# Routing the first share of tokens in the drain of attention, with a larger share and blank matmuls in every step

## The chip, the cores and the metric

The kernel runs on one core of one Trainium2 chip. The metric is device time in microseconds (us) of one execution, the median of several runs. A difference under about 2% (11 us here) counts as no difference.

## The reference

Sixteen sequences of 256 tokens with 128 features go through one post-norm attention layer with 16 heads of 8 features, and then through a mixture of experts, each with a residual and a layer norm.

```python
q, k, v = heads(x @ Wq.T + bq), heads(x @ Wk.T + bk), heads(x @ Wv.T + bv)
attn = softmax(q @ k.T / sqrt(8)) * head_mask
x = layernorm(x + (attn @ v) @ Wo.T + bo)              # x: 16 x 256 x 128
probs = softmax(x @ Wr)                                # 8 experts
gate = top-2 of probs, divided by their sum
routed = sum over e of (gelu(x @ Wfc[e] + bfc[e]) @ Wproj[e] + bproj[e]) * gate[:, e]
shared = gelu(x @ Wfc_s + bfc_s) @ Wproj_s + bproj_s
x = layernorm(x + shared + routed)
```

The kernel computes only the two chosen experts of each token: the token's row is sent to two slots of a table in HBM, sorted by expert, and the expert stage works through that table.

## The kernel before

Four stages follow each other, each with its own instruction queues and a barrier of all engines between them.

**Attention** (`build_attention`). One batch is one sequence. A software pipeline of 20 steps (`STEPS = BATCHES + 4`, t = 0 to 19) works on several batches at once. In step t the batch `now` = t-1 has its raw scores made by TensorE and its row maxima taken by VectorE (`largest`, 16 reductions, L554). The batch `late` = t-2 has its shifted scores made by TensorE, into a ring of two PSUM buffers (`ring_ps`), and exponentiated by ScalarE (`exp_pair`, 8 of them). The batches `last` = t-3 and `gone` = t-4 are normalised, projected and put through the layer norm (`add_residual`, `take_stats`, `take_mean` on VectorE, `make_x1` on GpSimd). The order on every engine is written out by hand, as a step function; TensorE's runs over eight pairs p = 0 to 7 of heads. Everything that uses the ring takes its place in it in TensorE's order: an entry can begin when the entry two places before has been evacuated by ScalarE. From step 17 on no batch is `now` (no maxima), from step 18 on none is `late`; steps 17 to 19 are called the drain here.

In between stands work for the second half of the layer. In odd steps GpSimd cuts four finished tiles of 128 tokens (`halve`), in even ones from 6 to 18 TensorE turns them (`turn`, p = 2) and makes their router logits (`find_logits`, p = 6). `keep_clock(n)` puts n blank matmuls of 512 columns in TensorE's queue, behind the projection of v at p = 2 and behind `turn_heads` at p = 6 in the steps of `KEPT`, and at other places in steps 0 to 2 and in the drain.

**Routing** is done by share (`SHARES`, in tiles; share 0 within attention, share 1 in the next stage). `Router.pick` finds the two best experts, TensorE counts the tokens of each expert (`share_counts`), `reserve` and `rank` turn counts into slots, `gate` makes the weights, `place` gives each token's slot, `shift_on` and `end_on` carry the state to the next share. All are small VectorE instructions, each of which waits for the one before it (`then`). `Placer.send` then issues one indirect DMA from GpSimd for each tile and each of the two choices (L1357), 64 in all. `PLACED` says how many go out within attention, at two places of a step; the rest go in the next stage.

**Shared expert** (`share_and_place`). TensorE, ScalarE and VectorE do the shared expert's 32 tiles (VectorE: `low`, L1534, and `add`, L1539). GpSimd does nothing but the sends that are left. The stage ends when every one of the 64 has landed.

**Routed experts** (`routed_experts`), 39 blocks of 256 slots, and **add and normalise**.

Of the kernel before, what the change touches and what calls it, by code (L numbers as in the profile page):

```python
# [14 lines left out]
HEADS = 16  # L15
# [17 lines left out]
SHARES = ((0, 16), (16, 32))  # L33
PICK_STEP, COUNT_STEP, PLACE_STEP = 13, 14, 15
TURNED_EARLY = 7
PLACED = {15: (0, 3), 16: (2, 3), 17: (2, 3), 18: (2, 2)}
# [4 lines left out]
KEPT = range(13, 17)  # L41
STEPS = BATCHES + 4
PROBS = 6
Q_AT, K_AT, TURN_AT, LOGIT_AT, COUNT_AT = 0, 3, 2, 6, 1
# [15 lines left out]
def ring_order():  # L60

    at = {("q", 0): 0, ("k", 0): 1}
    for t in range(STEPS):
        for p in range(PAIRS):
            if Batch(t - 2).exists():
                at["pair", t - 2, p] = len(at)
            if p == COUNT_AT and t == COUNT_STEP:
                at["counts", 0] = len(at)
# [29 lines left out]
def build_attention(nc, a):  # L98

    ctx = ExitStack()  # L100
    with ctx:
# [304 lines left out]
        def _(act):  # L406
# [72 lines left out]
            def step(t):  # L479
# [7 lines left out]
                if t == COUNT_STEP:  # L487
                    take_counts(0)
# [26 lines left out]
                if t == COUNT_STEP:  # L515
                    share_gap(nc, act, a, 0)
# [17 lines left out]
        def _(dve):  # L534
# [62 lines left out]
            def step(t):  # L597
                now, last, gone = Batch(t - 1), Batch(t - 3), Batch(t - 4)
                if now.exists():
                    largest(now, 0)  # L600
                    largest(now, 1)
# [12 lines left out]
                if now.exists():  # L614
                    largest(now, 4)
                    largest(now, 5)
                if t == PICK_STEP:
                    logits_taken(0)
                    router.find(0, 0)
                if t == COUNT_STEP:  # L620
                    counts_taken(0)
                    router.tally(0)
                if t == PLACE_STEP:
                    router.place(0, 0)
                if now.exists():
                    largest(now, 6)
                    largest(now, 7)
                if t == PICK_STEP:
                    router.mark(0)
                if t == COUNT_STEP:  # L630
                    router.claim(0)
                if t == PLACE_STEP:
                    router.place(0, 1)
# [3 lines left out]
                if now.exists():  # L637
                    largest(now, 8)
                    largest(now, 9)
                if t == PICK_STEP:  # L640
                    router.settle(0, 0)
                if t == COUNT_STEP:
                    router.offset(0)
                if t == PLACE_STEP:
                    router.shift_on(0)
                if now.exists():
                    largest(now, 10)
                    largest(now, 11)
                if t == PICK_STEP:
                    router.find(0, 1)  # L650
                if t == COUNT_STEP:
                    router.order(0)
                if t == PLACE_STEP:
                    router.end_on(0)
                if now.exists():
                    largest(now, 12)
                    largest(now, 13)
                if t == PICK_STEP:
                    router.mark(0)
                if t == COUNT_STEP:  # L660
                    router.jump(0)
                if now.exists():
                    largest(now, 14)
                    largest(now, 15)
                if t == PICK_STEP:
                    router.settle(0, 1)
                if t == COUNT_STEP:
                    router.gate(0)
# [4 lines left out]
        def _(pe):  # L673
# [134 lines left out]
            def step(t):  # L808

                ahead, new, now, late, last, gone = (Batch(t - back) for back in range(-1, 5))  # L810
                for p in range(PAIRS):
# [19 lines left out]
                    if p == COUNT_AT and t == COUNT_STEP:  # L831
                        count(0)
# [38 lines left out]
                    elif p == 4 and now.exists():  # L871
                        keep_clock(3)
                    if p == 5:
# [54 lines left out]
FIRST_TILES = 48  # L928
# [245 lines left out]
class Router:  # L1174
# [151 lines left out]
    def end_on(self, c):  # L1326
# [6 lines left out]
        then(nc.vector.tensor_copy(a["free"][:, c + 1], a["passing"][:, c, EXPERTS - 1:EXPERTS]))  # L1333

# [611 lines left out]
```

How the kernel before makes its waits and increments, by code:

```python
        @block.sync  # L220
# [1 line left out]
            def load_xt(b):  # L222
                if b.n >= 3:
                    sp.wait_ge(v_projected, b.n - 2)
                sp.dma_start(x_t[:, b.n % 3], a["x_t"][:, b.n * SEQ:(b.n + 1) * SEQ]).then_inc(xt_in[b.n % 3], 16)
            load_xt(Batch(0))
            for tile, name in ((wq, "wq_t"), (wk, "wk_t"), (bq, "bq"), (bk, "bk")):
                sp.dma_start(tile[:], a[name]).then_inc(qk_weights_in, 16)
            load_xt(Batch(1))
            for tile, name in ((bv, "bv"), (wo, "wo_t"), (wv, "wv_t")):
                sp.dma_start(tile[:], a[name]).then_inc(weights_in, 16)
            sp.dma_start(mask_col[:], a["mask"].unsqueeze(1).to_broadcast([HEADS, DH])).then_inc(weights_in, 16)
            sp.dma_start(bo_row[:], a["bo"].partition_broadcast(P)).then_inc(bcast_in, 16)
            sp.wait_ge(k_cleared, 1)
            def load_max(b, half):
                sp.wait_ge(max_evacuated, 2 * b.n + half + 1)
                rows = BANDS // 2 * IN_BAND * TILES
                for part in range(MAX_PARTS):
                    row = half * (BANDS // 2) * BAND + TERM_ROWS + part
                    sp.dma_start(q_stack[row:row + BAND + 1:BAND, b.par].rearrange("k g (t q) -> k (g t) q", t=TILES),
                                 max_t[part * rows:(part + 1) * rows, half, :]).then_inc(max_in[half], 16)
# [86 lines left out]
            def add_bias(b):  # L332
                pool.wait_ge(x_loaded[b.par], 16 * (b.half + 1))
                if b.n >= 1:
```

## Time and profile before

| | us |
|---|---|
| three runs | 545.31, 546.8, 557.79 |
| median | 546.8 |
| the profiled execution | 545.12 |
| its span, first to last instruction | 543.4 |

The span is 1.7 us shorter than the time of the same execution; the rest lies around it. The profiled execution is 1.7 us faster than the median. Times below count from the start of the span. In the trace attention ends at about 288 us, the shared expert at about 358, the routed experts at about 500. Step t of attention is taken from the first row maximum of its batch to that of the next.

### The profile page before, as it was taken

To read this page: it belongs to the slowest core of one execution; us is meant where nothing else is said; L and a number is where in the kernel's file an instruction comes from. 1 tells how busy PE (TensorE), PEld (TensorE's weight loads), DVE (VectorE), ACT (ScalarE), POOL (GpSimd) and SP (SyncE) were. 2 spreads that over 40 slices of the span, in tenths; PEclk is the share of its full clock that TensorE was granted. 3 is DMA by queue.
4 is the path that set the end of the run, shared out by engine and by line. 5 is a ranking of instruction groups with operands and counts; after the bars stand their busy time and mean duration, and the time that the engine had idled before them with its cause. 6 is when DMAs were issued, how large, how long until landed. Compare 5 with 4: busy or idle time off the path is not lost. (4 is left out here: it accounts for less than half of the span.)

```text
span 543.4 us, 14332 instructions
## 1 busy us (share of the span) xinstructions
PE 439.7 (81%) x5151; PEld 300.1 (55%) x5151; DVE 374.3 (69%) x857; ACT 306.3 (56%) x546; POOL 324.0 (60%) x433
## 2 busy tenths in 40 slices
PE   5999989999999898899976599926999999994000
PEld 2444445455555454444545489924999999993000
DVE  3558768687888789978322765513899998983095
ACT  1147868687878887657635457712545454541035
POOL 5402586556484766357886778830466666667185
PEclk9999879798999999959997799976999999998555
DMA  3223454445445452622111111119311111100453
GB/s 89 78 80 99 125 148 109 124 110 163 113 137 140 141 159 63 157 62 67 46 55 44 56 51 41 47 45 300 86 47 45 46 46 35 36 27 22 149 207 108
DMA packets 63127, 50.29 MB, mean 93 GB/s; under 512 B 7354, under 2 KB 54596, under 8 KB 63060
## 3 DMA queue, kind: packets, MB, share of 16 engines
q1 hardware_dynamic: 58516, 40.91, 26.9%
q0 software_dynamic: 4544, 8.47, 4.9%
q8 instruction: 44, 0.72, 0.6%
q14 instruction: 23, 0.19, 0.1%
HBM read 24.96 MB, written 22.95 MB: 88 GB/s over the span
## 5 line engine op out<-in xcount | busy, mean ns | idle before, releaser
L554 DVE TENSOR_REDUCE row_max<-s_ps 128x2 f32<-128x512 f32 x256 | 164.8, 683 | 47.9 <-PE s_ps L712 45.2
L413 ACT ACTIVATE probs<-ring_ps 128x1024 f32<-128x1024 f32 x128 | 130.9, 1023 | 59.4 <-PE ring_ps L730 59.2
L1653 POOL DMA_INDIRECT results<-gated,dest x78 | 78.8, 1010 | 64.3 <-DVE gated L1754 51.1
L1725 ACT ACTIVATE hid_r<-h_ps_r,bias 128x256 f32<-128x256 f32 x156 | 61.1, 474 | 74.2 <-PE h_ps_r L1390 74.2
L712 PE MATMUL s_ps<-qk_stack 24*128 24x256 f16 x512 | 89.7, 282 | 11.8 <-DVE row_max L554 5.1
L730 PE MATMUL ring_ps<-qk_stack 26*128 26x256 f16 x512 | 89.3, 283 | 0.0
L1357 POOL DMA_INDIRECT slots<-rows,slot_at x64 | 71.0, 1110 | 20.8 <-issue 18.1
L748 PE MATMUL av_ps<-probs,v_aug 128*32 128x256 f32 x1024 | 74.3, 411 | 0.0
L712 PEld LDWEIGHTS s_ps<-qk_stack 24*128 24x128 f16 x512 | 34.8, 95 | 69.4 <-issue 24.5
L1402 PE MATMUL y_ps_r<-w,hid_r 128*128 x312 | 58.2, 220 | 0.0
L1403 PE MATMUL y_ps_r<-w,hid_r 128*128 x312 | 57.9, 219 | 0.0
L1401 PE MATMUL y_ps_r<-w,hid_r 128*128 x312 | 57.6, 220 | 0.0
L316 POOL TENSOR_SCALAR max_scaled<-row_max 128x16 f32<-128x16 f32 x32 | 6.6, 205 | 72.8 <-DVE row_max L554 72.3
L1765 DVE SCALAR_TENSOR_TENSOR hid_r<-hid_r 128x1024 f16<-128x1024 f32 x39 | 47.8, 1225 | 1.3
L1388 PE MATMUL h_ps_r<-rows,w 128*128 128x256 f16 x156 | 43.5, 279 | 2.4 <-DVE rows L1744 2.4
L1534 DVE SCALAR_TENSOR_TENSOR hid<-hid 128x512 f16<-128x512 f32 x32 | 22.2, 693 | 31.6 <-ACT hid L1507 31.1
L748 PEld LDWEIGHTS av_ps<-probs,v_aug 128*32 128x32 f32 x1024 | 28.1, 115 | 28.3 <-issue 13.2
L1389 PE MATMUL h_ps_r<-rows,w 128*128 128x256 f16 x156 | 43.5, 279 | 0.0
L1390 PE MATMUL h_ps_r<-rows,w 128*128 128x256 f16 x156 | 43.4, 278 | 0.0
L1762 DVE TENSOR_SCALAR hid_r<-hid_r 128x1024 f16<-128x1024 f32 x39 | 27.0, 693 | 14.6 <-ACT hid_r L1725 14.5
L730 PEld LDWEIGHTS ring_ps<-qk_stack 26*128 26x128 f16 x512 | 34.7, 95 | 2.2 <-issue 1.7
L695 PE MATMUL ring_ps<-blank 128*128 128x512 f16 x115 | 32.8, 411 | 1.3 <-ACT probs L413 1.3
(208 smaller groups left out, 1046.5 us busy)
## 6 DMA issues: line engine op xcount, KB each, us to landing
qk_stack<-qk_rows SPq DMA_DIRECT2D x64, 96.0 KB
slots<-empty_row SPq DMA_DIRECT2D x13, 390.0 KB, 5.3
qk_rows<-qk_parts SPq DMA_DIRECT2D x16, 256.0 KB, 2.6
experts<-results SPq DMA_DIRECT2D x8, 512.0 KB, 6.9
rows_in<-slots SPq DMA_DIRECT2D x3, 1040.0 KB, 12.5
w_stage<-in_w_fc SPq DMA_DIRECT2D x9, 256.0 KB, 3.1
w_stage<-in_w_proj SPq DMA_DIRECT2D x9, 256.0 KB, 3.4
x_t<-in_x_t SPq DMA_DIRECT2D x16, 128.0 KB, 2.2
```

The costliest lines, as they stand in the source:

```text
L413: nc.scalar.activation(probs[:, n % PROBS], ring(key), ACT.Exp, scale=SCORE_SCALE).then_inc(ring_emptied, 1)
L554: nc.vector.tensor_reduce(row_max[:, h], s1_ps[:, h % 2], AX_X, ALU.max, negate=True).then_inc(max_done, 1)
L712: mm = nc.tensor.matmul(s1_ps[:, h % 2, t], band_of(q_stack, b, h, TERM_ROWS)[:, t * P:(t + 1) * P], band_of(k_stack, b, h, TERM_ROWS), st ...
L730: mm = nc.tensor.matmul(ring(("pair", b.n, p))[:, n % 2, t], band_of(k_stack, b, h, rows)[:, t * P:(t + 1) * P], band_of(q_stack, b, h, ro ...
L748: mm = nc.tensor.matmul(av_ps[32 * j:32 * j + 32, r], v_aug[:, b.par, t, s * HALF + r * 4 + j], probs[:, (PAIRS * b.n + 2 * n + j // 2) % ...
L1357: nc.gpsimd.indirect_dma_start(out=a["slots"][:, :], out_offset=bass.IndirectOffsetOnAxis(ap=a["slot_at"][:, k, tile:tile + 1], axis=0), i ...
L1401: nc.tensor.matmul(y_ps, h_hi[:, units], one_of(w16[:, 0], e, lo, hi), start=False, stop=False)
L1402: nc.tensor.matmul(y_ps, h_hi[:, units], one_of(w16[:, 1], e, lo, hi), start=False, stop=False)
L1403: mm = nc.tensor.matmul(y_ps, h_lo[:, units], one_of(w16[:, 0], e, lo, hi), start=False, stop=(c == CHUNKS - 1))
L1653: nc.gpsimd.indirect_dma_start(out=a["results"][:, :], out_offset=bass.IndirectOffsetOnAxis(ap=dest[:, t.buf, half:half + 1], axis=0), in_ ...
L1725: act_ = nc.scalar.activation(hid[:, t.buf % 2, cols], h_ps[:, t.buf % 2, cols], ACT.Gelu_apprx_tanh, scale=1.0 / UNIT, bias=bias[:, t.buf ...
L1765: nc.vector.scalar_tensor_tensor(out=hid16[:, t.buf, 1], in0=hid[:, t.buf % 2], scalar=X_UNIT, in1=hid16[:, t.buf, 0], op0=ALU.mult, op1=A ...
```

## The change

1. Share 0 grows from 16 tiles to 24, share 1 shrinks from 16 to 8.
2. Share 0's routing leaves steps 13 to 15, where its parts stood between the row maxima of a loaded VectorE. It now stands in step 17 (`pick`, counts, `reserve`, `rank`) and step 18 (`gate`, `place`, `move_on`). With 24 tiles an instruction over all tiles has 192 elements per partition and not 128. Its counts on TensorE move from p = 1 of step 14 to p = 5 of step 17, and ScalarE takes them there.
3. Of the 64 sends 17 stood in steps 15 to 18; now 4 do, at the end of step 18. The next stage has 60 and not 47.
4. `KEPT` is steps 3 to 16 and not 13 to 16: four more blank matmuls in each of steps 3 to 12, 40 in all.

```diff
-SHARES = ((0, 16), (16, 32))
-PICK_STEP, COUNT_STEP, PLACE_STEP = 13, 14, 15
+SHARES = ((0, 24), (24, 32))
+ROUTE_STEP = 17
-PLACED = {15: (0, 3), 16: (2, 3), 17: (2, 3), 18: (2, 2)}
+PLACED = {18: (0, 4)}
-KEPT = range(13, 17)
+KEPT = range(3, 17)
-Q_AT, K_AT, TURN_AT, LOGIT_AT, COUNT_AT = 0, 3, 2, 6, 1
+Q_AT, K_AT, TURN_AT, LOGIT_AT, COUNT_AT = 0, 3, 2, 6, 5
...
 # ScalarE, between exp_pair(late, 5) and exp_pair(late, 6)
-                if t == COUNT_STEP:
+                if t == ROUTE_STEP:
+                    take_counts(0)
                     share_gap(nc, act, a, 0)
...
 # VectorE
             def step(t):
+                if t == ROUTE_STEP:
+                    logits_taken(0)
+                    router.pick(0, 0)
                 # row maxima 0 to 3, add_residual, take_stats, take_mean
...
+                if t == ROUTE_STEP:
+                    router.pick(0, 1)
+                if t == ROUTE_STEP + 1:
+                    router.gate(0)
                     router.place(0, 0)
                 if last.exists():
                     invert_sums(last)
                     normalise(last)
...
+                if t == ROUTE_STEP:
+                    counts_taken(0)
+                    router.reserve(0)
+                    router.rank(0)
+                if t == ROUTE_STEP + 1:
+                    router.place(0, 1)
+                    router.move_on(0)
...
-FIRST_TILES = 48
+FIRST_TILES = 66
```

The removed lines between the row maxima of steps 13 to 15, one for each part of the routing, are left out. `FIRST_TILES` is the number of slot tiles that must have been emptied before share 0's first send.

GpSimd's queue from the end of step 17 to nearly the end of attention, before (L1357 is a send, L347 to L352 are `make_x1`, L339 is `add_bias`):

```order
L1357 DMA slots<-rows,slot_at 9984x130 x5
L347 TENSOR_SCALAR var_eps<-mean_var 128x2
L349 TENSOR_TENSOR rstd<-var_eps,minus_half 128x2
L352 TENSOR_SCALAR x_all<-z,mean_var,rstd 128x128 x2
L339 TENSOR_TENSOR xb<-x_in,out_bias 128x256
L1357 DMA slots<-rows,slot_at 9984x130 x2
L347 TENSOR_SCALAR var_eps<-mean_var 128x2
L349 TENSOR_TENSOR rstd<-var_eps,minus_half 128x2
L352 TENSOR_SCALAR x_all<-z,mean_var,rstd 128x128 x2
```

The same place now (L1330 is the send):

```order
L347 TENSOR_SCALAR var_eps<-mean_var 128x2
L349 TENSOR_TENSOR rstd<-var_eps,minus_half 128x2
L352 TENSOR_SCALAR x_all<-z,mean_var,rstd 128x128 x2
L339 TENSOR_TENSOR xb<-x_in,out_bias 128x256
L1330 DMA slots<-rows,slot_at 9984x130 x4
L347 TENSOR_SCALAR var_eps<-mean_var 128x2
L349 TENSOR_TENSOR rstd<-var_eps,minus_half 128x2
L352 TENSOR_SCALAR x_all<-z,mean_var,rstd 128x128 x2
```

The five sends ahead of the last but one `make_x1` are gone; ahead of the last one stand four and not two.

VectorE's queue in step 18 now, from the layer norm's statistics of batch 14 (L586) to the normalisation of batch 15 (L561, L565); before, these three rows followed each other with nothing between:

```order
L586 BN_AGGR mean_var<-stats 128x2 x2
L1209 TENSOR_SCALAR gate<-exp_gap 128x24
L1210 RECIPROCAL gate<-gate 128x24
L1211 TENSOR_TENSOR rows<-gate,exp_gap 128x24
L1212 COPY rows<-gate 128x24
L1282 TENSOR_TENSOR over<-rank,hot 128x192
L1283 TENSOR_REDUCE first<-over 128x24
L1284 CAST slot_at<-first 128x24
L561 RECIPROCAL sum_inv<-misc_ps 128x32
L565 TENSOR_TENSOR heads_out<-misc_ps,sum_inv 128x256
```

Seven routing instructions, `gate` and the first `place`, moved in between.

## Rows read from the trace of the kernel before

**Rows 1.** The page, part 2: busy tenths in 40 slices of 13.6 us.

```profile
PEclk9999879798999999959997799976999999998555
```

**Rows 2.** Busy time by window: steps 3 to 6, 8, 10, 11, 13 to 16.

```profile
core 0: us, PE busy (x) PEld busy (x) DVE busy (x) ACT busy (x) POOL busy (x), PEclk, DMA share, GB/s
47.10:62.80 15.70, 13.91 (x152) 7.10 (x148) 11.29 (x25) 12.29 (x18) 4.19 (x11) 0.89 0.52 148
62.80:78.40 15.60, 13.94 (x154) 6.95 (x150) 11.69 (x24) 11.45 (x17) 13.63 (x18) 0.92 0.45 125
78.40:93.40 15.00, 14.58 (x154) 7.65 (x150) 11.88 (x24) 11.28 (x17) 10.21 (x16) 0.86 0.31 84
93.40:110.70 17.30, 16.11 (x174) 8.74 (x170) 11.72 (x23) 11.66 (x18) 9.13 (x14) 0.80 0.45 127
...
124.00:139.70 15.70, 14.51 (x174) 8.20 (x170) 11.73 (x23) 11.66 (x18) 9.11 (x14) 0.89 0.52 147
...
153.00:167.60 14.60, 13.24 (x174) 7.48 (x170) 11.71 (x23) 11.54 (x18) 9.13 (x15) 1.00 0.61 160
167.60:181.30 13.70, 12.81 (x154) 6.64 (x150) 11.73 (x24) 11.38 (x17) 8.42 (x19) 1.00 0.55 151
...
195.90:212.40 16.50, 14.58 (x163) 7.53 (x160) 15.52 (x36) 12.14 (x18) 11.81 (x21) 1.00 0.40 108
212.40:229.70 17.30, 14.81 (x175) 7.65 (x174) 16.60 (x43) 11.78 (x22) 9.49 (x15) 0.99 0.48 124
229.70:247.30 17.60, 17.39 (x150) 7.80 (x148) 13.92 (x35) 10.54 (x15) 8.92 (x15) 0.62 0.22 58
247.30:261.70 14.40, 13.73 (x171) 7.25 (x167) 11.52 (x23) 10.92 (x16) 12.30 (x18) 1.00 0.20 60
```

**Rows 3.** The same view: the drain, the shared expert, the hand-over behind it.

```profile
261.70:288.20 26.50, 19.52 (x186) 11.21 (x185) 5.04 (x19) 11.10 (x15) 22.35 (x31) 0.99 0.15 46
289.80:358.50 68.70, 59.62 (x854) 53.95 (x854) 40.42 (x108) 44.39 (x72) 53.83 (x47) 0.89 0.16 50
358.50:368.00 9.50, 0.59 (x4) 0.35 (x4) 0.00 (x0) 0.00 (x0) 0.00 (x0) 0.53 0.33 85
```

**Rows 4.** The sends of the shared stage, in two windows: ns min/median/max, first and last start.

```profile
L1357 POOL DMA_INDIRECT slots<-rows,slot_at x27: 954/958/1423, 290.5 to 325.5; - x27
L1357 POOL DMA_INDIRECT slots<-rows,slot_at x20: 957/1307/1314, 326.8 to 357.4; - x20
```

**Rows 5.** Timeline, GpSimd and VectorE at full pace: start, us, engine, line, operation.

```profile
345.91 0.69 DVE L1534 SCALAR_TENSOR_TENSOR hid<-hid 128x512 f16<-128x512 f32 x1 [0.73 <-ACT hid L1507]
346.12 1.31 POOL L1357 DMA_INDIRECT slots<-rows,slot_at  x1 [0.30 <-issue]
```

**Rows 6.** Waits in 96 to 100 us: total, times, longest.

```profile
PEld ring_ps L763 <- ACT x L452: 0.9, 1, 0.9
```

**Rows 7.** Timeline of the drain.

```profile
266.52 1.04 PE L695 MATMUL ring_ps<-blank 128*128 128x512 f16 x4 [0.80 <-ACT probs L413]
...
278.87 0.36 DVE L562 RECIPROCAL sum_inv<-misc_ps 128x32 f32<-128x32 f32 x1 [1.63 <-PE misc_ps L775]
...
282.45 0.96 POOL L1357 DMA_INDIRECT slots<-rows,slot_at  x1 [0.30 <-issue]
...
283.07 0.25 DVE L587 BATCH_NORM_AGGREGATE mean_var<-stats 128x2 f32<-128x6 f32 x2
...
283.49 0.19 POOL L347 TENSOR_SCALAR var_eps<-mean_var 128x2 f32<-128x2 f32 x1
```

**Rows 8.** Timeline of VectorE: share 1's routing in the shared stage.

```profile
297.53 0.29 DVE L1224 TENSOR_TENSOR hot<-score,first 128x128 f32<-128x128 f32 x1
297.86 0.29 DVE L1206 SCALAR_TENSOR_TENSOR rest<-hot,logits 128x128 f32<-128x128 f32 x1
...
304.01 0.42 DVE L1253 TENSOR_TENSOR_SCAN up_to<-not_first,in_tile 128x128 f32<-128x128 f32 x1
...
308.44 0.29 DVE L1302 TENSOR_TENSOR rank<-rank,over 128x128 f32<-128x128 f32 x1
```

More of the change, by code:

```diff
@@ L66, in ring_order @@
                 at["pair", t - 2, p] = len(at)
-            if p == COUNT_AT and t == COUNT_STEP:
+            if p == COUNT_AT and t == ROUTE_STEP:
                 at["counts", 0] = len(at)
@@ L486, in step @@
                     exp_pair(late, 1)
-                if t == COUNT_STEP:
-                    take_counts(0)
                 if late.exists():
@@ L514, in step @@
                     evacuate_max(now, 0)
-                if t == COUNT_STEP:
+                if t == ROUTE_STEP:
+                    take_counts(0)
                     share_gap(nc, act, a, 0)
@@ L614, in step @@
                 if now.exists():
[L615 to L623, printed above, removed]
-                    router.place(0, 0)
[L625 to L633, printed above, removed]
+                    for h in range(4, 8):
+                        largest(now, h)
+                if t == ROUTE_STEP:
+                    router.pick(0, 1)
+                if t == ROUTE_STEP + 1:
+                    router.gate(0)
+                    router.place(0, 0)
                 if last.exists():
@@ L637, in step @@
                 if now.exists():
[L638 to L668, printed above, removed]
+                    for h in range(8, HEADS):
+                        largest(now, h)
+                if t == ROUTE_STEP:
[5 more added lines that the diff above has]
+                    router.move_on(0)
             run_steps(step)
@@ L830, in step @@
                             project("q", ahead, wq)
-                    if p == COUNT_AT and t == COUNT_STEP:
-                        count(0)
                     if p == 1:
@@ L872, in step @@
                         keep_clock(3)
+                    if p == COUNT_AT and t == ROUTE_STEP:
+                        count(0)
                     if p == 5:
@@ L1333, in end_on, with move_on @@
         then(nc.vector.tensor_copy(a["free"][:, c + 1], a["passing"][:, c, EXPERTS - 1:EXPERTS]))
+    def move_on(self, c):
+        self.shift_on(c)
+        self.end_on(c)
 class Placer:
```

## The prediction

> **What bounds the kernel now.** I read the busy tenths first, then windows cut at the steps, then the sends. In attention no engine is idle for long, and the clock line dips four times in slices 4 to 9 (counted from 0), deepest in slice 17, and again behind attention [rows 1]. The windows say which steps pay. An undisturbed step with weights to cast and without rows to turn (step 11) takes 13.7 us at full clock, one with rows to turn (step 10) 14.6 us; VectorE is busy for 11.7 us in either, TensorE for 12.8 and 13.2 [rows 2]. Both are close to the bound: TensorE's queue runs in order and waits for a row maximum here and an evacuation there. Steps 13 and 14 take 16.5 and 17.3 us at full clock, with VectorE busy for 15.5 and 16.6: there the routing makes VectorE the bound. Step 15 takes 17.6 us at a mean clock of 0.62, so about (1 - 0.62) / 0.5 = 76% of it ran at 1.2 GHz.
>
> The next stage is the point of the whole change. The shared expert keeps TensorE busy for 59.6 of 68.7 us, but the stage ends with a send: 47 sends, the first at 290.5, the last at 357.4 and 0.96 long, so 67.9 us [rows 3, 4]. Two things end together there, and GpSimd's queue of sends is a bound already. Behind it stand the landing, the barrier and the load of the slots, with next to nothing on any engine [rows 3].
>
> **Part 1: the routing leaves steps 13 to 15.** It is 15.5 + 16.6 + 13.9 - 3 x 11.7 = 10.9 us of VectorE [rows 2]. Step 13 should fall to step 11's 13.7 plus blanks (it had them already; 0.5 us, part 2) = 14.2: 2.3 us. Step 14 falls from 17.3 to 14.6 + 0.5 = 15.1: 2.2 us. Step 15 has no projections of q and k; at full clock I take 13.2 us: 4.4 us. The slow clock there came behind step 14, in which TensorE was kept waiting by VectorE; with that cause gone I expect full clock. Step 16 (14.4 us, blanks and rows to turn, no routing) stays. Sum **-9 us**, bounds -11 (all of VectorE's time comes off) and -5 (the dip stays).
>
> **Part 2: 40 blank matmuls in steps 3 to 12.** Four stand in 1.04 us, the last one's tail included, so one is about 0.22 us [rows 7]: 0.85 us of TensorE per step at full clock. Steps 13 to 16 already had them. Step 16 with them takes 14.4, step 10 without them 14.6, but step 16 lacks the two projections, which I put at a bit over 1 us; some of the blanks thus lies in waits that TensorE has anyway, such as that for ScalarE's evacuation of the turned rows (0.9 us) [rows 6]. I take 0.5 us a step, 5 us; ends 0 and 8.5. On the other side the clock: the windows of steps 3, 4, 5, 6 and 8 have 0.89, 0.92, 0.86, 0.80 and 0.89, together 20 us at 1.2 GHz, and take 79.3 us where clean ones would take 3 x 13.7 + 2 x 14.6 = 70.3: 9 us. Blanks at p = 2 and p = 6 stand at the waits behind which the clock fell in steps 6 and 8, less so in step 4; I let them save 6.5 of the 9. Sum **-1.5 us**, from -9 (blanks free, clock held) to +8.5 (blanks in full, clock no better).
>
> The Trainium skill, page "TensorE: Matmul & The Clock Gate", section "Terms", puts the penalty of throttled time at that time times (1 - K/N); for 20 us at half rate that is an estimate of 10 us, where the rows give 9. By it the best case of this part would be 1 us better; the trace agrees within that.
>
> **Part 3: the drain.** VectorE has only 5.0 us of work in 26.5 there, TensorE 19.5 [rows 3], so most of the routing finds room, but some stands ahead of what the drain's chain waits for. Dependent instructions over 128 elements follow at 0.33 us (297.53, 297.86), those over 8 take 0.17 against 0.29 [rows 8]; per element 0.001 us, so 0.39 us over 192. `pick` is 13 of them, 5 us, split around the statistics of batch 13; the first half delays these by 0.15 us, the second is done before TensorE reaches p = 5. The two count matmuls and ScalarE's two copies and one exponential, some 0.3 us each, enter the ring between pairs 5 and 6 and push the last three exponentials back by about 0.6 us. `reserve` and `rank` took 4.7 us for 128 elements [rows 8], so 5.2 here, from the counts (about 271.9) to 277.0: the residual of batch 14 waits 0.4 us for them. `gate` and `place` (7 instructions, 1.9 us) end at about 280.2, where `normalise` of batch 15 could begin at 278.9 before [rows 7]: 1.3 us late in all. That is on the path to the last `make_x1`.
>
> GpSimd adds more. The first slots are known at 280.2 and four sends go out from about 281.7 at 0.96 + 0.30 = 1.26 us each [rows 5, 7], to 286.7. The last `make_x1` stands behind them; it began at 283.5, just behind a send that ended at 283.4 [rows 7]. So the drain ends 3.3 us later; without the four sends it would be 1.3. Bounds +1 and +6, since tensor operations of VectorE and GpSimd's may meet. **+3.3 us.**
>
> **Part 4: 60 sends in the shared stage and not 47.** This decides. A send is 0.96 us and 0.30 us of issue, 1.26 in all [rows 4, 5]. Of the 67.9 us for 47 sends 47 x 1.26 = 59.2 are this; 8.7 us are sends that took longer. They are those that meet L1534: at full pace a send starts 0.21 us behind L1534 and takes 1.31 us, and the sends then follow each other at (357.4 - 326.8) / 19 = 1.61 us [rows 4, 5], one per tile of the shared expert. TensorE's tiles do not get more, so neither do these meetings: the 13 further sends come when VectorE is done, and each costs 1.26 us. 13 x 1.26 = **+16.4 us**; nothing covers them, since TensorE has no work left. Bounds: +8 if no send met VectorE at all (60 x 1.26 = 75.6 against 67.9), +21 if all 13 were stretched to 1.61. Share 1's routing with 8 tiles is about 25 instructions shorter by 0.07 us, but VectorE does not end the stage. The hand-over behind the last send stays.
>
> The Trainium skill, page "SBUF — State Buffer", section "Who interferes with whom", says that a VectorE instruction with two SBUF inputs contends with a GpSimd one that reads SBUF, and that whichever starts first keeps the shared port until it is done. L1534 reads two such inputs, and the trace agrees (1.31 against 0.96 us). The page speaks against moving sends into this stage, and against routing beside `make_x1` in the drain, as the upper bound of part 3 has it.
>
> **Sum.** -9 - 1.5 + 3.3 + 16.4 = +9.2 us against the profiled 545.1: 554.3 us. That execution was 1.7 us under the median of 546.8; I name **555 us**, between the sum on the one and on the other. A difference under 2%, 10.9 us, is not told from none.
>
> **Rivals.**
> (a) *The blanks hold the clock for nothing.* Part 2 gives -9 and not -1.5: 547 us. For it: every dip lies in a step without blanks or with VectorE as bound. Against it: TensorE is busy for 12.8 of 13.7 us already.
> (b) *The sends lose their meetings.* If a better clock and a shorter share 1 let VectorE finish early, or the sends slip between: part 4 gives +8 to +10, 547 us. Against it: the lock at 1.61 us held for 19 sends.
> (a) and (b) together: about 539 us; a few more microseconds would be needed for 2% faster.
> (c) *Slower: blanks without the clock.* The place is p = 2 and p = 6 of steps 3 to 12. Blanks cost 0.85 us each step and the low stretches remain or move: part 2 gives +8.5, 564 us. It decides from +2 us on in part 2, where the sum crosses 557.7. For it: the drops of step 4 came behind waits at which no blank stands.
> (d) *The drain's chain*: VectorE's routing and GpSimd delay each other and part 3 gives +6 to +8: 558 us.
> (e) *The change doesn't do what it says*: the low stretch of step 15 stays (part 1 gives -5): 559 us.
>
> **How the numbers follow.** The forecast, 550 to 557.7 us: 0.55. (a) or (b): 0.17. Both, and more: 0.03. (c): 0.12. (d) or (e): 0.13. From these: faster by over 2% 0.03, within 2% 0.69 (the forecast, (a) or (b), hardly any of the others), slower by over 2% 0.28, as the forecast lies only 3 us from that line and some of its own spread crosses it. The range 547 to 562 us leaves out the double gain and most of (c).
>
> **What the profile after would show.** Right: `PLACED`'s four sends just ahead of the last `make_x1`; 60 sends in the shared stage over 83 to 86 us, the last dozen at 1.26 us with TensorE idle; steps 13 to 15 at 13 to 15 us and full clock; attention about 8 us shorter up to step 17. The prediction is wrong if the sends of the shared stage take under 80 us, if the steps 3 to 12 lose or gain more than 8 us together, or if TensorE and not a send ends the shared stage.

## The result, and the profile after

| | before | after |
|---|---|---|
| median of 8 runs, us | 548.1 | 552.8 |
| lowest to highest, us | 545.3 to 563.6 | 549.8 to 563.1 |
| the profiled execution, us | 545.12 | 557.09 |
| its span, us | 543.4 | 555.3 |

The ratio is 1.0115 with a 95% interval of 1.0078 to 1.0153: the change costs 4 to 8 us, under the 2% that counts as a difference. The two profiled executions lie further apart (11.9 us in span), because that of before was 3 us under its median and that of after 4 us over its own.

Medians here and below are of all runs, but a ratio and its interval are taken only from runs within 1.5% of the fastest of their kernel, so the two can point different ways.

The experiments were measured in four series, each with the kernel before beside it. In the first two (the first eight experiments) every kernel, the one before too, took about 70 us more: 40 to 49 of them in the shared expert and 21 to 26 behind it, by their profiles (TensorE crawled there, see the last section). So each experiment is compared with the kernel before of its own series.

The time went as follows, stage by stage, in the profiled executions (a step is again taken from first row maximum to first row maximum):

| us | before | after | difference | forecast |
|---|---|---|---|---|
| steps 3 to 12 | 148.8 | 151.4 | +2.6 | -1.5 |
| steps 13 to 15 | 51.4 | 41.9 | -9.5 | -9 |
| step 16 to the first send of the shared stage | 43.2 | 45.5 | +2.3 | +3.3 |
| first to last send of that stage | 67.8 | 83.5 | +15.7 | +16.4 |
| the rest | 232.2 | 233.0 | +0.8 | 0 |
| span | 543.4 | 555.3 | +11.9 | +9.2 |

The page after, part 2, the line that answers to [rows 1], and GpSimd's; slices of 13.9 us:

```profile
POOL 5312665656565767454477788740366666667185
PEclk9999976999999999999968999655999999999555
```

One dip is left in attention where there were several: slices 5 and 6. The dip of slice 17 is gone. GpSimd's line holds 7 or 8 from slice 20 up to slice 25, which ends at 361 us, and 4 in the next, while the clock line is at 6 and 5 there: sends run on and TensorE has nothing.

Windows of the kernel after, at its own steps 4, 5, 9, 10, 13, 14 and 15; they answer to [rows 2]:

```profile
core 0: us, PE busy (x) PEld busy (x) DVE busy (x) ACT busy (x) POOL busy (x), PEclk, DMA share, GB/s
...
61.20:78.20 17.00, 14.81 (x160) 7.38 (x154) 11.75 (x23) 11.48 (x17) 14.30 (x21) 0.91 0.49 138
78.20:97.30 19.10, 19.10 (x158) 9.54 (x154) 11.95 (x23) 11.81 (x17) 10.04 (x15) 0.64 0.24 62
...
140.90:154.50 13.60, 13.17 (x158) 6.91 (x154) 11.75 (x23) 11.41 (x17) 7.92 (x16) 1.00 0.37 104
154.50:169.50 15.00, 14.00 (x178) 7.88 (x174) 11.71 (x23) 11.76 (x18) 9.36 (x16) 1.00 0.59 156
...
198.10:211.70 13.60, 13.17 (x158) 6.91 (x154) 11.75 (x23) 11.41 (x17) 11.10 (x18) 1.00 0.36 104
211.70:226.70 15.00, 14.00 (x178) 7.89 (x174) 11.71 (x23) 11.76 (x18) 9.37 (x16) 1.00 0.49 139
226.70:240.00 13.30, 12.71 (x154) 6.18 (x150) 11.53 (x24) 10.70 (x15) 6.21 (x14) 1.00 0.34 91
```

Steps 13 to 15 are now as quick as steps 9 and 10, with VectorE at 11.5 to 11.8 us in each and the clock at 1.00. What is left of the low clock stands in steps 4 and 5, 17.0 and 19.1 us; from step 6 to step 14 the even ones take 15.0 and the odd ones 13.6. Before, step 4 took 15.6 and step 5 15.0.

The same view, the shared stage up to TensorE's end, the sends behind it, the hand-over; they answer to [rows 3]:

```profile
285.50:349.00 63.50, 56.49 (x852) 51.32 (x851) 38.28 (x107) 43.70 (x72) 50.18 (x44) 0.94 0.16 51
349.00:369.00 20.00, 0.22 (x4) 0.04 (x1) 0.29 (x1) 0.00 (x0) 15.30 (x16) 0.56 0.16 53
369.00:378.70 9.70, 0.03 (x1) 0.06 (x2) 0.00 (x0) 0.00 (x0) 0.01 (x1) 0.50 0.20 48
```

For 20 us GpSimd is the only engine with work: 16 sends and nothing else.

What follows the stage is the load of the slots. TensorE's first matmul of the next stage waits for it. The waits (total, times, longest) of the kernel before in 350 to 368 us, and of the kernel after in 340 to 380:

```profile
PE t_ps L1679 <- DMA rows_in<-slots: 9.6, 1, 9.6
```

```profile
PE t_ps L1652 <- DMA rows_in<-slots: 29.4, 1, 29.4
```

Before, TensorE's last matmul (357.5) and the last send (358.4) ended within 0.9 us of each other, and the landing, the barrier and the load took 8.7 us behind the send. After, they take 9.7 us (369.0 to 378.7), and TensorE waits for the sends as well, 29.4 us in all.

The sends of this stage in three windows (ns min/median/max, first and last start), as [rows 4]:

```profile
L1330 POOL DMA_INDIRECT slots<-rows,slot_at x26: 954/959/1411, 285.5 to 318.9; - x26
...
L1330 POOL DMA_INDIRECT slots<-rows,slot_at x18: 1268/1307/1315, 320.1 to 347.5; - x18
...
L1330 POOL DMA_INDIRECT slots<-rows,slot_at x16: 954/958/959, 349.1 to 368.1; - x16
```

Eighteen sends are locked to VectorE's `low` (L1507 now) at (347.5 - 320.1) / 17 = 1.61 us, as twenty were before; the sixteen behind them go at (368.1 - 349.1) / 15 = 1.27 us.

GpSimd's timeline of the drain (start, us, engine, line, operation), as [rows 7]:

```profile
274.46 1.24 POOL L1330 DMA_INDIRECT slots<-rows,slot_at  x1 [0.19 <-issue]
...
278.53 0.95 POOL L1330 DMA_INDIRECT slots<-rows,slot_at  x1 [0.30 <-issue]
279.56 0.19 POOL L347 TENSOR_SCALAR var_eps<-mean_var 128x2 f32<-128x2 f32 x1
...
283.05 1.16 POOL L1088 TENSOR_TENSOR rows<-x_all,rows 128x512 f16<-128x512 f32 x1
285.53 1.12 POOL L1330 DMA_INDIRECT slots<-rows,slot_at  x1 [1.33 <-POOLq L101]
```

The four sends stand just ahead of the last `make_x1`. Counted from the start of step 16 (240.0; 247.3 before) this `make_x1` begins at 39.6 us and not at 36.2: 3.4 us later. The 36.2 is the best that before's routing and sends gave: in the other four profiles with both (experiments below) the clock was low in step 16 or in the drain, and it was 39.0, 39.1, 44.5 and 44.6.

### The profile page after: what moved, and what is told of

Read it like the earlier page. It is cut to its first block and busy times, and to the rows that moved or that the text cites. A ratio compares the mean times of both kernels' runs of the same rounds, so it can differ in the third digit from the quotient of the medians.

```text
span 555.3 us, 14405 instructions
## 1 busy us (share of the span) xinstructions
PE 435.8 (78%) x5191; PEld 298.7 (54%) x5191; DVE 375.0 (68%) x857; ACT 307.6 (55%) x546; POOL 322.6 (58%) x433
## 5 line engine op out<-in xcount | busy, mean ns | idle before, releaser
L680 PE MATMUL s_ps<-qk_stack 24*128 24x256 f16 x512 | 85.7, 277 | 6.8 <-DVE row_max L553 2.4
L698 PE MATMUL ring_ps<-qk_stack 26*128 26x256 f16 x512 | 85.2, 277 | 0.0
L1330 POOL DMA_INDIRECT slots<-rows,slot_at x64 | 69.6, 1088 | 20.4 <-issue 19.1
L716 PE MATMUL av_ps<-probs,v_aug 128*32 128x256 f32 x1024 | 71.1, 397 | 0.0
L680 PEld LDWEIGHTS s_ps<-qk_stack 24*128 24x128 f16 x512 | 34.6, 93 | 62.9 <-issue 32.2
L1738 DVE SCALAR_TENSOR_TENSOR hid_r<-hid_r 128x1024 f16<-128x1024 f32 x39 | 47.8, 1225 | 1.3
L663 PE MATMUL ring_ps<-blank 128*128 128x512 f16 x155 | 44.3, 399 | 1.3 <-ACT probs L413 1.3
L1507 DVE SCALAR_TENSOR_TENSOR hid<-hid 128x512 f16<-128x512 f32 x32 | 22.2, 693 | 30.6 <-ACT hid L1480 30.2
L1652 PE MATMUL t_ps<-ident_h,rows_in 128*128 128x128 f16 x156 | 15.9, 227 | 31.8 <-DMA rows_in<-slots 31.8
```

The source lines that it names most:

```text
L680: mm = nc.tensor.matmul(s1_ps[:, h % 2, t], band_of(q_stack, b, h, TERM_ROWS)[:, t * P:(t + 1) * P], band_of(k_stack, b, h, TERM_ROWS), st ...
L698: mm = nc.tensor.matmul(ring(("pair", b.n, p))[:, n % 2, t], band_of(k_stack, b, h, rows)[:, t * P:(t + 1) * P], band_of(q_stack, b, h, ro ...
L716: mm = nc.tensor.matmul(av_ps[32 * j:32 * j + 32, r], v_aug[:, b.par, t, s * HALF + r * 4 + j], probs[:, (PAIRS * b.n + 2 * n + j // 2) % ...
L1330: nc.gpsimd.indirect_dma_start(out=a["slots"][:, :], out_offset=bass.IndirectOffsetOnAxis(ap=a["slot_at"][:, k, tile:tile + 1], axis=0), i ...
L1738: nc.vector.scalar_tensor_tensor(out=hid16[:, t.buf, 1], in0=hid[:, t.buf % 2], scalar=X_UNIT, in1=hid16[:, t.buf, 0], op0=ALU.mult, op1=A ...
```

## The experiments

### Are the sends what costs, and why 83.5 us?

**Three runs of the kernel before with the sends alone moved**: its routing and its `KEPT` stay.

```diff
-PLACED = {15: (0, 3), 16: (2, 3), 17: (2, 3), 18: (2, 2)}
+PLACED = {18: (0, 4)}
```

> The kernel before with only the table of sends changed: four at the end of step 18 and 60 in the shared stage, routing still in steps 13 to 15 with 16 tiles. Theory (the sends are the price, 1.26 us each once VectorE is done): the shared stage's sends take 84 us and not 68, the whole 16 us more, 563 to 565. Rival (sends alone do not set the end of that stage, the late routing or the drain does): under 556.

> The same kernel as in the third experiment (the kernel before, with four sends in attention and 60 in the shared stage), since in that run, and in all of its call, a stretch from the drain on waited for something outside the kernel. Theory (the sends are the price): 60 sends take 84 us from first start to last end, the whole is 16 us over before, 562 to 564. Rival (sends alone do not set the end of that stage): under 556.

> The kernel before with only the table of sends changed (four in attention, 60 in the shared stage), in the state of the chip in which the result was measured. Theory: 60 sends take 84 us and not 68, the drain is 1 us longer, the whole 16 to 17 us over before, 564. Rival (sends alone do not set the end of that stage): under 556.

Medians against before of the same series: 642.8 against 627.3 (too few comparable runs for an interval), 629.6 against 616.2 (ratio 1.0215 [1.0149, 1.0282]), and 571.7 against 549.0 (1.0384 [1.0310, 1.0457]). Slower each time, by 13 to 23 us; but in the first two the crawling TensorE ended the stage, 42 to 44 us behind the last send, so only the third tests what the sends do. Of it, windows of a stretch of attention, of the shared stage up to TensorE's end and of what follows:

```profile
73.00:134.50 61.50, 61.34 (x436) 30.82 (x436) 33.80 (x66) 33.75 (x50) 28.13 (x48) 0.50 0.31 85
309.30:375.40 66.10, 57.34 (x852) 51.92 (x851) 40.27 (x107) 43.73 (x72) 52.20 (x46) 0.93 0.16 51
375.40:392.90 17.50, 0.23 (x5) 0.06 (x1) 0.29 (x1) 0.00 (x0) 13.40 (x14) 0.54 0.16 53
```

The sends take 309.3 to 392.9, that is 83.6 us, as in the kernel after. So the number of sends in the stage makes its length, and neither the routing nor the blanks does. The 21 to 23 us in all are more than the 16 expected; in this execution, the longest of its kernel, attention had the clock at 1.2 GHz for 61.4 us in one piece (first row), which the edit doesn't touch directly. Whether the few sends taken out of steps 15 to 17 have a part in this, no run tells.

**The changed kernel with `low` reading PSUM.** The gelu's result is written back to its PSUM buffer, so that `low` has one operand in SBUF and not two. The computation is the same.

```diff
-                    pe.wait_ge(activated, n - 3)
+                    pe.wait_ge(hidden_low, n - 3)
...
-                nc.scalar.activation(hid[:, n % 4], h_ps[:, n % 4], ACT.Gelu_apprx_tanh, scale=1.0 / UNIT).then_inc(activated, 1)
+                nc.scalar.activation(h_ps[:, n % 4], h_ps[:, n % 4], ACT.Gelu_apprx_tanh, scale=1.0 / UNIT).then_inc(activated, 1)
...
-                nc.vector.scalar_tensor_tensor(out=hid16[:, n % 4, 1], in0=hid[:, n % 4], scalar=X_UNIT,
+                nc.vector.scalar_tensor_tensor(out=hid16[:, n % 4, 1], in0=h_ps[:, n % 4], scalar=X_UNIT,
```

> The changed kernel; in the shared expert ScalarE writes its gelu back into the PSUM tile and not into SBUF, so that VectorE's low part (the instruction that the stretched sends meet) reads one operand from PSUM and one from SBUF. The result is computed as before. Theory (a VectorE instruction with two SBUF operands holds off a send): all 60 sends take 1.26 us, 76 us in all and not 83.6, and the whole is 7 to 8 us faster than the changed kernel, 545. Rival (a send is stretched for another reason, for instance VectorE's or ScalarE's writes to SBUF): 83 to 84 us for the sends and no gain.

> The changed kernel with gelu written back into PSUM, once more: in the first run of it TensorE crawled while the sends were issued, in this kernel and in the kernel before alike, which hid what the edit does to the pace of the sends. Theory (a VectorE instruction with two SBUF operands holds off a send): 60 sends in 76 us and not 83.6, 7 to 8 us faster than the changed kernel, level with the kernel before. Rival (a send is stretched for another reason): 83 to 84 us and 1% over the kernel before.

The first time, with TensorE crawling, the stage did not end with the sends and the edit could not show: 615.6 against 616.2 (1.0003 [0.9958, 1.0049]). The second time: **546.1 against 547.6, 0.9992 [0.9941, 1.0043]**, where the change without this edit has 1.0115 [1.0078, 1.0153]. Both are ratios to the kernel before, of different series; the intervals don't meet, and the edit gives about 7 us. Its sends, in two windows (the one at 321.2 stands in both), and the windows of the stage up to TensorE's end and of the sends behind it:

```profile
L1330 POOL DMA_INDIRECT slots<-rows,slot_at x31: 954/958/1638, 282.4 to 321.2; - x31
...
L1330 POOL DMA_INDIRECT slots<-rows,slot_at x30: 954/958/961, 321.2 to 357.8; - x30
```

```profile
281.80:345.50 63.70, 56.11 (x853) 50.76 (x854) 38.59 (x107) 42.68 (x72) 48.17 (x50) 0.95 0.18 57
345.50:358.80 13.30, 0.22 (x4) 0.04 (x1) 0.29 (x1) 0.00 (x0) 10.21 (x11) 0.64 0.16 53
```

The longest send of the second half takes 961 ns, where the locked eighteen took 1307. Sixty sends need 358.8 - 282.4 = 76.4 us and not 83.5, with TensorE's part no shorter (63.7 against 63.5). In the trace of before a send that starts 0.21 us behind L1534 takes 0.35 us more than one alone [rows 4, 5]; take the second SBUF operand away and this is gone.

The edit takes more away than that operand: ScalarE's write of the gelu to SBUF goes with it, and could be the cause instead (VectorE's own write to SBUF stays). The traces say no. The last stretched send of before has VectorE's `low` beside it and nothing of ScalarE:

```profile
355.57 0.69 DVE L1534 SCALAR_TENSOR_TENSOR hid<-hid 128x512 f16<-128x512 f32 x1 [0.72 <-ACT hid L1507]
355.79 1.30 POOL L1357 DMA_INDIRECT slots<-rows,slot_at  x1 [0.30 <-issue]
```

And the stretch follows VectorE to the hundredth. In the profiles of before, of after and of the third run with the sends moved, 74 sends start 0.10 to 0.53 us behind the start of a `low`, and each ends 0.83 us behind that `low`'s end, however much of it was left: these sends stand still until VectorE is done. The three that start within 0.02 us of it take 0.96 us. In the three profiles outside the crawling series with gelu in PSUM, 58 sends start while a `low` runs, and none takes over 0.96 us. The one send of 1.64 us in the first window above started behind another VectorE instruction with two SBUF operands (L1518, on one partition), and it ends 0.84 us behind it:

```profile
306.55 0.87 DVE L1518 TENSOR_TENSOR passed<-number,passing 1x704 f32<-1x704 f32 x1
306.62 1.64 POOL L1330 DMA_INDIRECT slots<-rows,slot_at  x1 [0.30 <-issue]
```

The Trainium skill, page "SBUF — State Buffer", section "Who interferes with whom", says that VectorE's second SBUF input comes through the interface that GpSimd reads by, and that one with at most one such input doesn't contend; this experiment agrees. The same section infers that `tensor_tensor` takes only the read interface while descriptor generation needs the write interface; for these indirect sends, which read their slots from SBUF, the 7.1 us say otherwise of an instruction with two SBUF inputs, and the send of 1.64 us says it of a `tensor_tensor` itself.

**The same edit on the kernel before.**

> The kernel before with the same edit. Theory: its 47 sends take 59 us and not 68, so that TensorE's tiles end the stage, at some 66 us: 2 us faster than before, 545. Rival (sends still stretched): no difference. If the stage's TensorE part is slower with gelu in PSUM, slower by that.

> The kernel before with gelu written back into PSUM. Theory: 47 sends take 59 to 60 us and not 68, so that TensorE's tiles end the stage at 62 to 66 us: 2 to 5 us faster than before, 543 to 545. Rival (TensorE's tiles end it as late as the sends did): no difference.

618.2 against 616.2 (1.0063 [1.0008, 1.0118]) with TensorE crawling, and then 550.5 against 549.0, from too few comparable runs for an interval (the fastest ones are 538.2 and 543.7). Windows of the second, the shared stage up to TensorE's end and from there to the first matmul of the routed experts:

```profile
310.60:377.20 66.60, 58.02 (x853) 52.35 (x854) 39.91 (x107) 42.97 (x72) 46.05 (x47) 0.92 0.17 53
377.20:381.20 4.00, 0.27 (x5) 0.10 (x3) 0.29 (x1) 0.00 (x0) 0.00 (x0) 0.73 0.47 111
```

Here 47 sends take 60.4 us, from 311.2 to 371.6, and TensorE ends the stage, at 377.5. Behind its last matmul the hand-over takes 3.8 us. That this is TensorE's own hand-over, and not the sends', is shown by the crawling series: in all eight profiles the last send had ended 45 to 48 us before the next stage began, and the last matmul 3.7 to 3.8 us. Without the crawling the sends come close here too: the next stage begins 9.6 us behind the last of them, as long as their own hand-over takes in the changed kernel (9.7). So from the first matmul of the shared expert to the first of the routed ones it is 381.2 - 310.6 = 70.6 us, against 367.1 - 289.9 = 77.2 in the profile of before: 6.6 us less. The median doesn't show them. This profiled execution took 162.9 us for steps 3 to 12, 14 more than that of before; what the others took there isn't known, but the mean granted clock over its six runs is 0.880, against 0.895 over the eleven of before, which points to a lower clock outside this stage.

### What do the four sends cost in the drain?

**The changed kernel with none placed.**

```diff
-PLACED = {18: (0, 4)}
+PLACED = {}
```

> The changed kernel with no send in attention, all 64 in the shared stage. Theory: the drain ends 2 us earlier, since nothing stands ahead of the last make_x1, and the shared stage is 4 x 1.26 = 5.0 us longer (89 us): 3 us slower than the changed kernel, 556. Rival (the drain is late by VectorE's routing alone): 5 us slower, 558.

621.6 against 627.3 (1.0038 [0.9954, 1.0123]); with TensorE crawling the whole time can't show the expected 3 us. GpSimd's timeline, last `make_x1` and first send:

```profile
273.21 0.19 POOL L347 TENSOR_SCALAR var_eps<-mean_var 128x2 f32<-128x2 f32 x1 [3.48 <-DVE mean_var L586]
...
279.02 1.24 POOL L1330 DMA_INDIRECT slots<-rows,slot_at  x1 [1.17 <-issue]
```

Step 16 begins at 235.4 in it: `make_x1` stands at 37.8 us, between before's 36.2 and after's 39.6. So VectorE's routing costs 1.6 us (forecast 1.3) and the four sends 1.8 (forecast 2.0). The runs with the sends moved give nearly the same from the other side: the kernel before with these four sends has 38.4 in the two profiles with a clean drain, 2.3 us for the sends, which leaves 1.1 for the routing. Now the last `make_x1` waits for VectorE (L586) and not for a send.

### What do the blanks do?

**The changed kernel without the 40 blanks, and the kernel before with them.**

```diff
 # after
-KEPT = range(3, 17)
+KEPT = range(13, 17)
 # before
-KEPT = range(13, 17)
+KEPT = range(3, 17)
```

> The changed kernel with the 40 blank matmuls of steps 3 to 12 taken out again, everything else as changed. Theory (the forecast's part 2: blanks cost about 0.3 us in a clean step and save clock): steps 3 to 12 take some 149 us with three to five low stretches of the clock, and the time is 1 to 2 us above the changed kernel's 552.8. Rival 1 (blanks are a net loss, and the change is slower partly for them): 2 to 5 us below, 548 to 551. In both cases the shared stage still takes 83 to 85 us for its 60 sends and steps 13 to 15 about 13.3 to 15 us each.

> The kernel before with the blank matmuls in steps 3 to 16 as the only change. Theory: 1 to 2 us faster than before, 546.5; clean even steps 15.0 and not 14.6 us. Rival 1 (net loss): 3 us slower, 551. If blanks hold the clock for nothing: 7 us faster.

621.6 against 627.3 (0.9974 [0.9892, 1.0056]) and 622.8 against 627.3 (1.0038 [0.9970, 1.0107]). Both are compared with the kernel before, so only the second pair differs by the blanks alone, and its whole times don't separate. The windows do for a clean step. The changed kernel without blanks, at full clock, two windows of the length of its steps 9 and 10 (each laid 1 us behind the step's start):

```profile
137.10:150.40 13.30, 12.76 (x152) 6.64 (x150) 11.76 (x24) 11.43 (x18) 8.63 (x16) 1.00 0.39 103
150.40:165.20 14.80, 13.26 (x171) 7.62 (x170) 11.67 (x24) 11.51 (x19) 8.72 (x15) 1.00 0.59 162
```

13.3 and 14.8 us without, 13.6 and 15.0 with them: four blanks cost 0.2 to 0.3 us a step, about 2.5 us in ten steps and not 5. TensorE is busy for 0.4 to 0.7 us more, and about half of that lies in its waits.

The clock is another matter. Steps 3 to 12 of every profiled execution, and for how long the granted clock was 1.2 GHz in them:

| without blanks | steps 3 to 12, us | low, us | with blanks | steps 3 to 12, us | low, us |
|---|---|---|---|---|---|
| before | 148.8 | 20.5 | after | 151.4 | 17.1 |
| changed, no blanks | 145.0 | 6.8 | before with blanks | 151.5 | 17.1 |
| before, sends moved (1) | 162.6 | 54.6 | changed, none placed | 146.2 | 3.4 |
| the same (2) | 150.1 | 20.5 | changed, gelu in PSUM (1) | 151.4 | 17.1 |
| the same (3) | 165.5 | 61.4 | the same (2) | 147.4 | 10.2 |
| before, gelu in PSUM (1) | 163.1 | 54.6 | changed, weights split late | 150.1 | 13.7 |
| the same (2) | 162.9 | 54.6 | before, gelu in PSUM, blanks | 148.7 | 10.2 |
| mean | 156.9 | | mean | 149.5 | |

With blanks the clock falls once, in steps 3 to 5, and from step 6 to step 12 every step is clean, in seven executions of seven. Without them it may stay low or fall again: in four of seven it was low for 54 us and more. These four are also long executions of their kernels, three of them the longest and one the second longest; without them the mean of the first column is 148.0, below that of the second. The two columns also give the price. Without blanks, from 6.8 to 54.6 us low the steps grow from 145.0 to 162.6: 17.6 / 47.8 = 0.37 us for each us low. With blanks, from 3.4 to 17.1 us, from 146.2 to 151.4: 5.2 / 13.7 = 0.38. Reckoned back to no low clock at all these are 142.5 and 144.9, which gives the cost of the blanks a second time, 2.4 us. So the 40 blanks pay from some 7 us of low clock on that they prevent.

The blanks thus hold the clock behind step 5, but they don't prevent the drop of steps 3 to 5. Seven profiles don't tell how often an execution without them is a bad one; the mean granted clock, which stands on record for every run, tells more. Two pairs differ by the blanks alone. The kernel before has 0.870 with them (6 runs) and 0.852 without (11), the same with gelu in PSUM 0.902 with (6) and 0.880 without (6). So by both pairs the blanks do raise the clock. The times follow less clearly: the means of all runs are 3.4 and 5.2 us lower with blanks, where single runs of one kernel lie 8 to 22 us apart.

**GpSimd's cutting of the first weights put behind its other work in step 4**, a guess at what starts that drop: in the kernel after, TensorE waits there for GpSimd's `split_max`, longer than in the profile of before (1.1 us; in the other profiles of before's attention it is 1.8 to 2.0 as well), and the clock is low from 75.0 on. Waits in 68 to 96 us (total, times, longest):

```profile
PE misc_ps L723 <- POOL max_parts L320: 1.8, 1, 1.8
```

```diff
-                if t == SPLIT_AT[0]:
-                    split_biases(late)
-                if t in SPLIT_AT:
+                if t in SPLIT_AT and t != SPLIT_AT[0]:
                     split_weights(SPLIT_AT.index(t))
...
                     halve(halved_in(t))
+                if t == SPLIT_AT[0]:
+                    pool.wait_ge(xb_made, last.n + 1)
+                    split_biases(late)
+                    split_weights(0)
```

> The changed kernel; in step 4 GpSimd splits the biases and the first weights at the end of the step and not ahead of the maxima that TensorE waits for at p = 5. Theory (in the changed kernel the one low stretch of the clock, 17 us in steps 4 and 5, starts behind that wait of 1.8 us, at which no blank stands): step 4 takes 13.6 us and not 17, step 5 13.6 and not 15 to 19, and the whole is 4 to 8 us faster, 545 to 549. Rival (the clock falls at that time for another reason): step 4 gets 2 us shorter by the wait alone and a low stretch remains.

614.8 against 616.2 (1.0008 [0.9974, 1.0041]). Its steps 4 and 5:

```profile
61.90:75.90 14.00, 13.21 (x158) 6.99 (x156) 11.76 (x23) 11.42 (x17) 9.80 (x15) 1.00 0.54 153
75.90:96.50 20.60, 19.23 (x158) 9.38 (x156) 11.87 (x23) 11.68 (x17) 15.06 (x23) 0.67 0.30 81
```

Step 4 is clean, 14.0 and not 17.0 us, so the wait, and the drop behind it, were what made it long. But the drop comes all the same, one step later, behind the same kind of wait of 1.3 us, and step 5 takes 20.6. That a late GpSimd starts the drop is borne out for its place only; the two steps together take 34.6 us against 36.1. And it isn't the only start. Thirteen of the fourteen profiles have this wait, 1.1 to 2.0 us long, and a drop 0.7 to 2.3 us behind it. The fourteenth, the second run with gelu in PSUM, hasn't it: its clock fell in step 3, at 59.2, behind a wait of 0.94 us for ScalarE that every profile has and that only one other, that of before, shows a drop behind.

### The kernel before, with both edits that proved sound

Before's routing and sends, `low` with PSUM (the edit above) and `KEPT = range(3, 17)`:

> The kernel before with gelu written back into PSUM and the blank matmuls in steps 3 to 16; routing, shares and sends as before. This is the version to which the runs so far point. Theory (the 40 blanks cost 0.3 us in a clean step and keep the clock from falling in all but steps 4 and 5): 2 to 4 us faster than the same without blanks, 541 to 543, faster than both kernels. Rival 1 (blanks a net loss): 2 to 3 us slower than the same without them.

**546.2 against 549.0, 0.9873 [0.9781, 0.9966]**: faster than the kernel before, by an interval that reaches from 2 to 12 us, and the only version of the study of which that holds. The evidence is thin: the ratio rests on three of its six runs, and the medians of all lie 2.9 us apart. Its clock line, and the windows of the shared stage up to TensorE's end and of the hand-over:

```profile
PEclk9999969999999999965997979986999999998555
```

```profile
295.10:361.70 66.60, 58.08 (x854) 52.38 (x854) 39.90 (x107) 42.95 (x72) 45.90 (x47) 0.92 0.17 53
361.70:365.70 4.00, 0.18 (x4) 0.02 (x2) 0.29 (x1) 0.00 (x0) 0.00 (x0) 0.72 0.52 121
```

Stage and hand-over are again 365.7 - 295.1 = 70.6 us, 6.6 less than before, and the gain by the ratio is 7 us. The sizes agree, but the same 6.6 us stood in the run without blanks, whose median showed no gain; so the two edits together are faster by that interval, and their shares aren't shown. In the two profiled executions it doesn't show in the span (543.5 and 543.4), because steps 13 to 15 took 3.3 us more in this one and the drain 2.9 more.

## Why the prediction was right

The sum was 554.3 us, the value named 555, the median 552.8; the forecast case (550 to 557.7) came true, not a rival. The large terms, parts 1 and 4, hold in mechanism and size. That the sum comes within 2 us of the median is partly luck: part 2 missed by 4 us in the profiled execution, and single runs of either kernel lie 13 to 18 us apart.

**Part 1, -9 us: measured -9.5.** Step 13 took 13.6 (14.2 forecast), step 14 15.0 (15.1), step 15 13.3 (13.2). The step that carried most, "with that cause gone I expect full clock" in step 15, held in all six profiled kernels that route in step 17: steps 13 to 15 take 41.9 us in each. In all eight profiles that route in 13 to 15 the clock fell in step 14 or 15 and they take 51.3 to 55.3 us, with blanks or without. Rival (e) is out. The prediction took before's 51.4 from one profile, near the lower end of these; over executions the part is worth up to 13.4 us.

**Part 2, -1.5 us: +2.6 in the profiled execution.** Two terms were mis-sized. The clean cost was put at 0.5 us a step and is 0.25. The clock's gain was put at 6.5 of 9 us; in this execution one drop of 17.1 us stood where several had made 20.5, and 3.4 x 0.38 = 1.3 us came back. That makes +1.2; of the rest, 0.7 us is the longer wait of step 4 (1.8 against 1.1 us), and 0.7 stays open. "For it: the drops of step 4 came behind waits at which no blank stands", said of rival (c), was the right reading of where: the drop in steps 3 to 5 stays in all seven. Over executions the term is not one number, as the table shows. By the ratio the whole change costs +6.3 us (4.3 to 8.4); but parts 1 and 3 too differ by 4 and 8 us from profile to profile of before's code, so what is left for part 2 over executions can't be told from it.

**Part 3, +3.3 us: +2.3.** Up to the last `make_x1` it is +3.4, of 1.6 for the routing and 1.8 for the four sends; the forecast had 1.3 and 2. What it missed is that from there to the first send of the next stage it takes 6.0 us where it took 7.0. The first send's own wait behind the stage's start is 1.33 us after and 2.39 before:

```profile
290.50 1.11 POOL L1357 DMA_INDIRECT slots<-rows,slot_at  x1 [2.39 <-POOLq L101]
```

This follows the table of sends and not the routing: it is 2.39 in all five profiles with before's table, 1.33 in all eight with four sends at the end of step 18, three of which have before's routing, and 1.17 with none. Why, stays open. Over executions the part is hardly a cost at all: from the start of step 16 to the first send the five profiles with before's routing and sends take 43.2 to 51.6 us, mean 47.7, the five of the changed kernel with its four sends 45.5 to 47.2. The single profile that the sum starts from was the best of its kind.

**Part 4, +16.4 us: +15.7.** 83.5 us against 84.3. The decomposition held too: 47 x 1.26 us and 8.7 us of meetings before, 60 x 1.26 and 83.5 - 75.6 = 7.9 us of meetings after, and 76.4 when the meetings are taken away (75.6 forecast as the lower bound). "TensorE's tiles do not get more, so neither do these meetings" is what kept this at 1.26 a send and not at 1.61. That the sends alone make the stage is shown by the kernel before with its sends moved, 83.6 us. One step of the account of the bound was wrong, without harm to the sum: "Two things end together there". The last send and the last matmul did, within 0.9 us, but the next stage begins 8.7 to 9.9 us behind the last send and 3.8 behind the last matmul if that comes late enough. So the sends alone ended the stage, by 5 to 6 us. The sum was not hurt, since every further send came behind that; but rival (b), the sends losing their meetings, takes 6.6 us off this stage in the kernel before as well.

So the change pays 15.7 us in a queue that was already the bound for 9.5 us in VectorE's. The gain in attention is real and stays; it is given back, with more, one stage later.

## What to carry to other kernels

Before moving work into a stage, ask which queue ends it: GpSimd ended this one, behind it a hand-over 5 to 6 us longer than TensorE's, so each send moved there cost about its full 1.26 us (15.7 us for 13). If sends must share a stage with VectorE, give VectorE's long instructions one operand in PSUM: here each send that started 0.1 us or more behind a `low` with two SBUF operands, and well ahead of its end, stood still until it was done. A single profile of a clock drop says little: here steps 3 to 12 had 3 to 17 us of low clock with blanks and 7 to 61 without, so read several, and the granted clock of every run, before pricing blanks.

## What the hardware showed beside

**TensorE crawls beside the sends in some series.** In the first eight experiments, on two chips, matmuls of the shared expert that follow each other by 0.06 us elsewhere came some 1 to 1.4 us apart while GpSimd sent; the kernel before, measured beside them without a trace, took as much longer. One such execution (the changed kernel, weights split late), TensorE and the sends in the timeline, and the window of 48 us around:

```profile
312.51 0.96 POOL L1332 DMA_INDIRECT slots<-rows,slot_at  x1 [0.30 <-issue]
313.55 0.27 PE L1377 MATMUL y_ps<-w,hid 128*128 128x128 f16 x1 [1.02 <-issue]
313.78 0.96 POOL L1332 DMA_INDIRECT slots<-rows,slot_at  x1 [0.31 <-issue]
314.95 0.10 PEld L1378 LDWEIGHTS y_ps<-w,hid 128*128 128x128 f16 x1 [2.58 <-issue]
314.95 0.28 PE L1378 MATMUL y_ps<-w,hid 128*128 128x128 f16 x1 [1.14 <-issue]
```

```profile
293.00:341.00 48.00, 10.45 (x49) 4.63 (x48) 2.94 (x11) 5.21 (x7) 36.48 (x38) 0.51 0.16 53
```

49 matmuls in 48 us, against 38 sends at their usual 1.26. No semaphore holds TensorE there ("issue"), and within the stage it recovers when the sends end. The sixty sends took 88.7 us (12.1 of them one wait for VectorE) and TensorE's part 130, so the stage ended with TensorE. The routed experts are slower as well: there TensorE takes 148 to 153 us in these eight profiles and 128 to 130 in the other six, with a send of GpSimd for each of 78 tiles of results. Slow loading of code isn't seen: beside the sends the transfers of the queue that the trace calls "instruction" took 1.41 us (median of 2) in the kernel before with blanks, which crawled, and 1.41 (median of 6) in the kernel before. On one of the two chips a later series ran without the crawling (the second run with gelu in PSUM, 546.1 us), so neither the chip nor the program alone decides it; the cause stays open. It also hides what the change costs: the changed kernel's variants were level with the one before in those series, with TensorE and not the sends ending the stage. The stage was longest where it had most sends: TensorE's part was 130 to 138 us with 60 or 64, 114 to 115 with 47.

**The clock stays low under full load.** In the third run with the sends moved TensorE was busy for 61.34 of 61.50 us at 1.2 GHz before the clock rose (the first row shown for that run). The Trainium skill, page "TensorE: Matmul & The Clock Gate", section "Terms", puts the penalty at half of the time at half rate; the rows give 0.38 of the time, as worked out behind the table above. How long the low clock lasts in steps 3 to 12 varies by a factor of eighteen between executions of like code (3.4 to 61.4 us), and no row says why.
